# A graph network on one core: node table dropped, edge lists turned on TensorE, gathers issued in waiting pairs

## The reference, cut to what matters

```python
x = _layernorm(x + L0(x, edges))   # two attentions, then a dense update
x = _layernorm(x + L1(x, edges))   # attention with 12 heads of 64
x = _layernorm(x + L2(x, edges))   # normalised neighbour sum, W
x = _layernorm(x + L3(x, edges))   # two such sums, W1 and W2

def gat_conv(x, src, dst, W, a_src, a_dst, bias, H, C, n):    # twice in L0
    h = (x @ W).reshape(n, H, C)
    s_src = (h * a_src).sum(-1)
    s_dst = (h * a_dst).sum(-1)
    e = leaky_relu(s_src[src] + s_dst[dst], 0.2)
    emax = segment_max(e, dst, n)
    ee = exp(e - emax[dst])
    alpha = ee / segment_sum(ee, dst, n)[dst]
    return segment_sum(alpha[:, :, None] * h[src], dst, n).reshape(n, H * C) + bias
```

## Time and profile before

| | us |
|---|---|
| median of 3 runs | 4335.33 |
| the profiled execution | 4339.43 |
| its span, first to last instruction | 4337.6 |
| TensorE matmuls busy in the span | 3720.0 (86%) |
| VectorE | 2597.3 (60%) |
| ScalarE | 1178.5 (27%) |
| GpSimd | 625.8 (14%) |

### The profile page before, as it was taken

The page is one execution under the profiler, slowest core; times in us unless marked ns, Lnnn a source line. Parts: engine busy times, 40 slices in busy tenths (PEclk is TensorE's granted clock), DMA queues, the critical chain, the costliest instruction groups (busy, mean ns, idle before and its releaser), DMA issues. The chain is left out here.

```text
span 4337.6 us, 64010 instructions
## 1 busy us (share of the span) xinstructions
PE 3720.0 (86%) x21454; PEld 3436.2 (79%) x21454; DVE 2597.3 (60%) x4977; ACT 1178.5 (27%) x1691; POOL 625.8 (14%) x640
## 2 busy tenths in 40 slices
PE   6886999699799888026888699999699999699999
PEld 5886999599699544015888399999399999499999
DVE  4765886067142488275999377777244443377777
ACT  2221232122122344003555222222222222222222
POOL 5523000414400000512000400000400000400000
PEclk8987999799899999568999899999899999899999
DMA  4783566346333588116776544444644443666665
GB/s 102 127 189 111 181 192 191 95 133 206 112 104 112 159 250 247 24 55 186 246 251 237 207 155 166 173 172 145 223 161 173 170 167 128 210 220 231 225 225 184
DMA packets 370508, 742.21 MB, mean 171 GB/s; under 512 B 109269, under 2 KB 162215, under 8 KB 370368
## 3 DMA queue, kind: packets, MB, share of 16 engines
q1 hardware_dynamic: 275600, 503.06, 38.1%
q10 hardware_dynamic: 67584, 154.63, 9.1%
q0 software_dynamic: 27184, 82.71, 6.2%
HBM read 444.99 MB, written 301.21 MB: 172 GB/s over the span
## 5 line engine op out<-in xcount | busy, mean ns | idle before, releaser
L666 DVE TENSOR_TENSOR fr_lo<-fr_turned_ps,fr_hi 128x768 fp32r<-128x768 f32 x158 | 150.4, 952 | 339.4 <-ACT fr_hi L1009 331.4
L1139 PE MATMUL fr_prod<-fr_wu_hi,fr_hi 128*128 128x396 f32 x948 | 261.5, 356 | 19.4 <-issue 19.4
L1139 PE MATMUL fr_prod<-fr_wu_lo,fr_hi 128*128 128x396 f32 x948 | 254.2, 348 | 18.3 <-issue 18.3
L1139 PE MATMUL fr_prod<-fr_wu_hi,fr_lo 128*128 128x396 f32 x948 | 252.7, 346 | 18.6 <-issue 18.5
L1139 PE MATMUL fr_prod<-fr_w_hi,fr_hi 128*128 128x396 f32 x948 | 259.2, 354 | 8.8 <-issue 8.8
L1139 PE MATMUL fr_prod<-fr_w_lo,fr_hi 128*128 128x396 f32 x948 | 251.6, 346 | 13.8 <-issue 13.8
L1139 PE MATMUL fr_prod<-fr_w_hi,fr_lo 128*128 128x396 f32 x948 | 250.5, 345 | 11.3 <-issue 11.3
L1009 ACT ACTIVATE fr_hi<-fr_turned_ps 128x768 fp32r<-128x768 f32 x158 | 127.4, 806 | 472.1 <-PE fr_turned_ps L1123 309.6
L2116 DVE SCALAR_TENSOR_TENSOR c3a_y<-c3a_prod,dinv,next_const 128x768 f32<-128x768 f32 x79 | 80.4, 1018 | 289.3 <-PE c3a_prod L2270 289.3
L2270 PE MATMUL c3a_prod<-next_w_hi,c3a_hi 128*128 128x384 f32 x948 | 248.1, 342 | 0.0
L2270 PE MATMUL c3b_prod<-next_w_hi,c3b_hi 128*128 128x384 f32 x948 | 248.0, 342 | 0.0
(11 more groups left out here) (480 smaller groups left out, 8585.4 us busy)
## 6 DMA issues: line engine op xcount, KB each, us to landing
fr_ins<-in_x_dram SPq DMA_DIRECT2D x156, 384.0 KB
h<-fr_outs SPq DMA_DIRECT2D x78, 396.0 KB
u<-fr_outs SPq DMA_DIRECT2D x78, 396.0 KB
up_ut<-u SPq DMA_DIRECT2D x78, 396.0 KB
agg<-fr_zrow SPq DMA_DIRECT2D x78, 390.0 KB
hds_agg<-agg SPq DMA_DIRECT2D x78, 390.0 KB
x<-up_x_o ACTq DMA_DIRECT2D x78, 384.0 KB
hds_row<-x SPq DMA_DIRECT2D x78, 384.0 KB
```

Of the source, the lines that this page charges most:

```text
L666: v.tensor_tensor(lo[:, s2, :, :], turned_ps[:, 0:KC, :], hi[:, s2, :, :].bitcast(F32), ALU.subtract).then_inc(split_done, 1)
L1139: made = nc.tensor.matmul(prods[s2][:, bank, 0:c1 - c0], l[:, s2, s, :], w[:, s, c0:c1], start=(s == 0 and i == 0), stop=(s == KC - 1 and ...
```

## The change

1. The table `nodes`, its 40 gathers and their buffers go. Own loops and dinv of each node become columns 8 and 9 of sc1, so that the gathers of the scores bring them. `sc_o` gets a place for every tile. The rows of sc1 for tiles 0 to 17 are stored later, at SyncE's steps 61 to 78.
2. `sd_c` is not loaded. At `AT_LISTS` TensorE turns both columns of `sd_r`, and VectorE reads the lists from there.
3. In both attentions each pair of gathers of the scores (for a column of 128 edges by src and by dst) waits until the pair in front has landed.
4. `AT_A` goes from 90 to 98, `AT_B` from 127 to 138. The copies of dinv and own loops, and the transpose of these, move from `AT_OWN` into the first attention.

```diff
-AT_A, AT_B = 90, 127
+AT_A, AT_B = 98, 138
...
-    nodes = dram("nodes", (NT * P, 2))
-    sc1 = dram("sc1", (N, 8))
+    sc1 = dram("sc1", (N, 10))
...
 def store(t):
-    sp.dma_start(tile_rows(sc1, t), sc_o[0:n, slot, :, :].rearrange("p h k -> p (h k)")).then_inc(stored[slot], 16)
...
 def step(t):                      # SyncE
+    if AT_NODE + 7 <= t < NT + 4:
+        store_scores(t - 4)
+    if NT - AT_NODE - 3 <= t < NT:
+        store_scores(t - (NT - AT_NODE - 3))
+def store_scores(t):
+    sp.wait_ge(out_ready, 2 * t + 2)
+    sp.wait_ge(node_done, 1)
+    sp.dma_start(tile_rows(sc1, t), sc_o[0:rows_of(t), t, :]).then_inc(sc_stored, 16)
...
-bg.to(AT_NODE + 2)
-sp.wait_ge(node_done, 1)
-sp.dma_start(nodes.rearrange("(t p) k -> p t k", p=P), pt["node"][:, :, :]).then_inc(node_out, 16)
 bg.to(AT_RELOAD)
-sp.dma_start(pt["sd_c"][:, :, :], packed[P:P + NC * P, :].rearrange("(c p) w -> p c w", p=P)).then_inc(reloaded, 16)
...
                                   # GpSimd
-for c in range(SC):
-    rows_from(nodes, pt["nd_src"][:, c, :], g["src_i"][:, c:c + 1], nd_in)
-    rows_from(nodes, pt["nd_dst"][:, c, :], g["dst_i"][:, c:c + 1], nd_in)
...
+pool.wait_ge(sc_stored, 16 * NT)
 for c in range(SC):
-    rows_from(sc1, gt["from_src"][:, c, :], g["src_i"][:, c:c + 1], la.scores_in)
-    rows_from(sc1, gt["from_dst"][:, c, :], g["dst_i"][:, c:c + 1], la.scores_in)
+    if c:
+        pool.wait_ge(la.scores_in[(c - 1) % 2], 32 * ((c + 1) // 2))
+    rows_from(sc1, gt["from_src"][:, c, :], g["src_i"][:, c:c + 1], la.scores_in[c % 2])
+    rows_from(sc1, gt["from_dst"][:, c, :], g["dst_i"][:, c:c + 1], la.scores_in[c % 2])
...                                # the same for lb, from h2
                                   # VectorE
-dve.wait_ge(reloaded, 64)
+dve.wait_ge(reloaded, 48)
+dve.wait_ge(lists_up, 1)
-link(v.tensor_copy(g["src_i"][:, 0:NC], sd_c[:, :, 0]))
-v.tensor_copy(g["dst_i"][:, 0:NC], sd_c[:, :, 1]).then_inc(lists_done, 1)
+link(v.tensor_copy(g["src_i"][:, 0:NC], pb[:, 0:NC]))
+link(v.tensor_copy(pt["dst_c"][:, :], pb[:, 128:128 + NC]))
+v.tensor_copy(g["dst_i"][:, 0:NC], pt["dst_c"][:, :]).then_inc(lists_done, 1)
...
 bg.to(AT_A)
+dve.wait_ge(la.fetched, 1)
+link(v.tensor_copy(g["edge_dinv"][:, :], fs[:, :, 9]))
+link(v.tensor_copy(own_e[:, :], fd[:, :, 8]))
...
                                   # TensorE
+bg.to(AT_LISTS)
+pe.wait_ge(reloaded, 48)
+nc.tensor.transpose(pb[:, 0:NC], pt["sd_r"][:, :, 0], idn)
+nc.tensor.transpose(pb[:, 128:128 + NC], pt["sd_r"][:, :, 1], idn).then_inc(lists_up, 1)
```

More of the change, by code:

```diff
@@ L167, in build @@
         }
-        first_layers(nc, g, a, packed, agg, nodes, h1, sc1, h2, out2, u)
+        first_layers(nc, g, a, packed, agg, h1, sc1, h2, out2, u)
         g["alpha"], g["own_w"] = sb("alpha", [P, NC, H_MAX]), sb("own_w", [P, NC, H_MAX])
@@ L205, in rest_groups, with first_layers @@
                     body(k * 2 + j)
-def first_layers(nc, g, a, packed, agg, nodes, h1, sc1, h2, out2, u):
+def first_layers(nc, g, a, packed, agg, h1, sc1, h2, out2, u):
     with ExitStack() as ctx:
@@ L282, in prep_tiles @@
                 ("pad", [P, (NC + 2) * 2], F32),
-                ("sd_c", [P, NC, 2], F32), ("sd_r", [NC, P, 2], F32), ("prv", [NC, 1], F32), ("nxt", [NC, 1], F32),
+                ("dst_c", [P, NC], F32), ("sd_r", [NC, P, 2], F32), ("prv", [NC, 1], F32), ("nxt", [NC, 1], F32),
                 ("is_last", [NC, P], F32), ("end_r", [NC, P], F32), ("val", [NC, P], F32), ("carry_r", [NC, 1], F32),
-                ("tmp_c", [P, NC], F32), ("deg", [P, NT], F32), ("sq", [P, NT], F32), ("node", [P, NT, 2], F32),
+                ("tmp_c", [P, NC], F32), ("deg", [P, NT], F32), ("sq", [P, NT], F32),
                 ("all_f", [NC, 1], F32), ("all_b", [NC, 1], F32),
-                ("before", [P, P], F32), ("nd_src", [P, NC, 2], F32), ("nd_dst", [P, NC, 2], F32),
-                ("nst", [P, GROUP, 2, 2], F32), ("nix", [P, 2, GROUP], I32), ("scr_p", [P, 8], F32))}
+                ("before", [P, P], F32), ("scr_p", [P, 8], F32))}
         (w1t, w2x, att2), pt, gt = overlay("c", setup_tiles, late_tiles, graph_tiles)
@@ L318, in first_layers @@
                                                                   sem("counted"), sem("offset"), sem("ranks"))
-        packs, slots, hots, hist, deg_done, deg_root, node_done, node_out = (
-            sem("packs"), sem("slots"), sem("hots"), sem("hist"), sem("deg_done"), sem("deg_root"), sem("node_done"), sem("node_out"))
+        packs, slots, hots, hist, deg_done, deg_root, node_done, sc_stored = (
+            sem("packs"), sem("slots"), sem("hots"), sem("hist"), sem("deg_done"), sem("deg_root"), sem("node_done"), sem("sc_stored"))
         zeros, reloaded, rows_done, rows_up, lists_done = (sem("zeros"), sem("reloaded"), sem("rows_done"), sem("rows_up"),
                                                            sem("lists_done"))
-        nd_zero, nd_in, nd_rest, nd_copied, nd_fetched, own_up, own_done = (
-            sem("nd_zero"), sem("nd_in"), sem("nd_rest"), sem("nd_copied"), sem("nd_fetched"), sem("own_up"), sem("own_done"))
+        lists_up, own_done = sem("lists_up"), sem("own_done")
         class Layer:
             def __init__(self, tag):
-                self.zeroed, self.scores_in, self.fetched = sem(tag + "zeroed"), sem(tag + "scores_in"), sem(tag + "fetched")
+                self.zeroed, self.fetched = sem(tag + "zeroed"), sem(tag + "fetched")
+                self.scores_in = [sem(f"{tag}scores_in{j}") for j in range(2)]
                 self.scored, self.up, self.edges, self.edges_up = sem(tag + "scored"), sem(tag + "up"), sem(tag + "edges"), sem(tag + "edges_up")
@@ L347, in stored_by @@
         def stored_by(t):
-            return sum(64 if s < NT else 16 for s in range(t % UNROLL, t + 1, UNROLL))
+            return sum(48 if s < NT else 16 for s in range(t % UNROLL, t + 1, UNROLL))
         @block.sync
@@ L535, in fetch_rest @@
                 rest_groups(pool, g, body)
-            fetch_rest(la, sc1, gt["sst"], 0, 8)
-            pool.wait_ge(la.scores_in, 32 * SC)
+            fetch_rest(la, sc1, gt["sst"], 0, 10)
+            for j in range(2):
+                pool.wait_ge(la.scores_in[j], 16 * SC)
             nc.gpsimd.memset(gt["scr"][:, 1:2], 0.0).then_inc(la.fetched, 1)
@@ L580, in _ @@
             for c in range(SC):
-                rows_from(h2, kept_rows[:, c, 0, :], g["src_i"][:, c:c + 1], lb.scores_in)
-                rows_from(h2, kept_rows[:, c, 1, :], g["dst_i"][:, c:c + 1], lb.scores_in)
+                if c:
+                    pool.wait_ge(lb.scores_in[(c - 1) % 2], 32 * ((c + 1) // 2))
+                rows_from(h2, kept_rows[:, c, 0, :], g["src_i"][:, c:c + 1], lb.scores_in[c % 2])
+                rows_from(h2, kept_rows[:, c, 1, :], g["dst_i"][:, c:c + 1], lb.scores_in[c % 2])
             fetch_rest(lb, h2, stage, 192, 4)
-            pool.wait_ge(lb.scores_in, 32 * SC)
+            for j in range(2):
+                pool.wait_ge(lb.scores_in[j], 16 * SC)
             nc.gpsimd.memset(gt["scr"][:, 1:2], 0.0).then_inc(lb.fetched, 1)
@@ L811, in _ @@
             bg.to(AT_OWN)
[L812 to L817, removed]
             link(v.tensor_scalar(gt["pen_f"][:, :], g["same_f"][:, 0:4 * P], -1.0, NEG, ALU.add, ALU.mult))
@@ L834, in both_ways @@
                 dve.wait_ge(l.edges_up, k)
+                if l is la and k == 1:
+                    link(v.tensor_scalar(own_r[:, :], pb[0:NC, 384:384 + P], 1.0, None, ALU.add))
                 rf, rb = ((pen_rf, pen_rb) if is_max else (g["row_f"], g["row_b"]))
@@ L1196, in hop @@
                 pe.wait_ge(l.edges, k)
+                if l is la and k == 1:
+                    nc.tensor.transpose(pb[0:NC, 384:384 + P], own_e[:, :], ident[:, :])
                 nc.tensor.transpose(pb[0:H, 0:NC], gt["edge"][:, 0, 0:H], idn)
```

23 lines of the change are left out of this document (10 added, 13 removed).

## The result

The changed kernel takes 4210.25 us (median of 4 runs, 4207.33 to 4211.64); the kernel before, on the same chip, 4336.32 (4 runs, 4334.88 to 4338.44). The ratio is 0.9708 [0.9691, 0.9725]: 126 us less. Forecast were 4197 and a range of 4172 to 4245. The profiled execution has a span of 4205.6 us, 132.0 less than before, and a mean granted clock of 0.953 (0.939 before).

A forecast was written before the change was run, and what follows sets the result against it. Four holes, 164 us of a 4337.6 us span, where TensorE starves for x or gets instructions late, were taken to bound it. -33.1 -43.4 +5 -49.4 -38.5 +21 = -138.4 gave 4201, as a median 4197; range 4172 to 4245.

The forecast's parts named there:

- Part 1: Table of nodes dropped: its 8-byte store goes, -33 us; two more score columns cost 0, bound 2 us.
- Part 2: Gathers from the table of nodes dropped: the hole at 340 to 386 us goes, -43 us.
- Part 3: Edge lists turned on TensorE, near tile 31: reload gains 0, VectorE waits for the lists; +5 us, bounds 0 and 8.
- hole 1: TensorE's gap at 205 to 236 us, starving for x behind the 8-byte store of the table of nodes: 33 us.
- Part 4: Gather pairs wait in the first attention: 20 pairs fit up to 5.9 us each; cost 0, bound 2; 49 us returned.
- Part 5: Gather pairs wait in the second attention: 39 us returned, but at p = 4.75 us a pair TensorE waits, +21 us.
- Holes 3 and 4: TensorE's gaps at 774 to 825 and 1119 to 1160 us, instructions late beside back-to-back gathers: 49.4 and 38.5 us.
- Rival B: Pacing doesn't free TensorE's instruction supply, or only in part: 4316 us, half relieved about 4240; chance 0.20.
- hole 2: TensorE's gap at 340 to 386 us, beside back-to-back gathers from the table of nodes: 43.4 us.

The follow-up runs named there:

- run 10: Changed kernel with the store of 128 x 79 pieces of 8 bytes put back at tile 17, read by nobody: 4243.53 us, ratio 1.0088.
- run 1: Changed kernel without the waits between pairs of gathers, all else the same: 4267.62 us, 57 us above the changed kernel.
- run 4: Changed kernel plus 40 unread gathers of 128 rows without a pause in pass c3a, a loop: 4244.40 us, 34 us above the changed kernel.
- run 9: Changed kernel with the reload at tile 28 instead of 26 and the lists turned one tile earlier: 4204.58 us, ratio 0.9991, inconclusive.
- run 12: Changed kernel with a wait after every second pair, AT_A 93, reload at tile 28, lists turned one tile earlier: 4173.03 us, ratio 0.9924.
- run 2: Changed kernel with a wait only after every second pair, four gathers in a row: 4190.00 us, 20 us under the changed kernel.
- run 8: Changed kernel with the first attention from tile 96 instead of 98: 4198.77 us, ratio 0.9981.
- run 11: Changed kernel with a wait only after every fourth pair, eight gathers in a row: 4181.16 us, ratio 0.9938.
- run 3: Changed kernel with each pair waiting for the pair before the last, two pairs under way: 4212.64 us (4191.94 to 4223.05).
- run 5: Changed kernel plus 40 unread plain GpSimd transfers of 128 rows of 40 bytes in pass c3a, without waits: 4212.47 us, ratio 1.0010.
- run 7: Changed kernel plus 40 unread gathers of 64 rows each in pass c3a, without waits: 4210.89 us, ratio 1.0010.
- run 6: Changed kernel plus 40 unread gathers of 32 rows each in pass c3a, without waits: 4211.14 us, ratio 1.0009.

## Why the prediction was right, and where it was off

**Part 1, right.** SyncE no longer has a long load near 197 us, and tile 17 starts 7.18 us after tile 16. -33.3 us came against -33.1, and run 10 puts it back with one store.

**Part 2, right in size, its cause by likeness.** -43.4 us was taken. The gathers of the table were never tried with pauses. That they slowed TensorE as a train, and not in another way, is argued from their form (128 rows, 1.30 us apart), which is that of runs 1 and 4, and not shown. TensorE's first wait for "issue" came there at 340.64 us, after 8 gathers, where the others needed 12 to 14.

**Part 3, right.** +5 was taken, +5.5 came, and in the order foreseen: VectorE stands 3.93 us (forecast 4), its low part comes late, and the tiles 31 and 32 take 10.78 and 8.67 us.
```profile
300.73 0.06 DVE L708 MEMSET src_i<- 128x4 int32 x1 [3.93 <-PE fr_pb L1145]
...
310.11 0.94 DVE L648 TENSOR_TENSOR fr_lo<-fr_turned_ps,fr_hi 128x768 fp32r<-128x768 f32 x1
```

**Not foreseen: +4.0 us at tiles 26 and 27.** With hole 1 gone TensorE reaches the reload 35 us earlier, and the scatters that it waits for do not. SyncE stands from 250.68 to 260.42, with the loads of x queued behind:
```profile
250.27 0.41 SPq L401 DMA_DIRECT2D sc<-fr_sc_o  x1
260.42 0.30 SPq L418 DMA_DIRECT2D fr_sd_r<-packed  x1
```
```profile
264.64 0.56 DVE L633 BATCH_NORM_STATS2 fr_stats<-fr_ins 128x6 f32<-128x384 f32 x1 [7.76 <-DMA fr_ins<-in_x_dram]
```
```profile
270.12 1.51 PE L1105 MATMUL fr_turned_ps<-ident,fr_xn 128*128 128x128 f32 x6 [2.46 <-DVE fr_lo L648]
```
The prediction asked what was late next for the gathers, and not for this queue. Runs 9, 10 and 12 bear it out: with hole 1 back (run 10) the 4.0 us are gone, and with the reload two tiles later (runs 9 and 12) too. How much is lost varies from trace to trace, because the last scatter's issue ends anywhere from 253.4 to 263.8 us where there is no hole 1: in runs 1 and 2 it ended at 255.2 and 253.4, and nothing was lost; in run 8 at 263.8, and 5.0 us were.

**Part 4, right.** It was said that 20 pairs fit up to 5.9 us each. They took 5.05, and nobody waited. -49.5 us came against -49.4.

**Part 5, the step that was mis-sized.** Its form was right: one wait of VectorE at tile 138 (35.1 us long), and room for p = 3.8. I took a landing of 2.0 us and p = 4.75, and +21 us; p was 5.15 and the price 26.7 + 1.3 = 28.0 over steps of 7.18 (27.4 over the 7.61 and 7.35 that tiles 139 and 140 take in run 11 without the wait). The forecast's own sum, 14.0 + 20 p + 3.5 - 93.5, gives 27.0 with the measured p, and 29 with the 2 us at the low clock, so p accounts for the miss. By the sum of the forecast, 5.15 - 2.3 - 0.45 is a landing of 2.4 us. The waits of the list average 55.0 / 19 = 2.9 us with the start of the next issue in them, where the forecast had 2.45. Each 0.1 us of a landing is paid 20 times. The error was to think the stage as good as quiet, since it moves only x and u: that is 149 GB/s by the stretches table, and the other bound, 3.32 us behind four scatters, was nearer than it looked. The rule weighed there, a fixed 2.0 us of the Trainium skill, DMA: Bandwidth & Descriptors, "Anatomy of one DMA", would have made the part free. Waits of 2.4 to 4.2 us behind an issue of 1.0 in this stage speak against taking it for a transfer beside others.

**Holes 3 and 4, the mechanism.** Two statements stood in one sentence, "TensorE gets its instructions late while gathers come without a pause". What the trace shows of it, waits for "issue" that pauses take away, holds in runs 1, 2 and 11. That it is late because of fetching is refuted by run 4. The cure was forecast by likeness with stretches that have pauses, and not from a known cause; that the cause named beside it was wrong cost nothing here, which is luck. Rival B doubted the cure, and is refuted by the 102.00 of 102 us; its remark that the holes would have another cause than fetching was right.

**The sum.** Forecast were -138.4 us; the terms came to -33.3 - 37.9 - 49.5 - 37.5 + 28.0 = -130.2. With the 4.0 not foreseen that is -126.2. Of the 12.2 us between, 7.0 are part 5 and 4.0 the tiles 26 and 27. The span's -132.0 has 5.8 us more. 2.3 of them are at the start-up, for which I have no cause (tile 0 alone moves by up to 4 us from run to run), and 3.4 between tiles 86 and 122, of which 2.5 are the four steps moved out of that row. The medians differ by 126.1, so that the terms meet them so closely is in part luck.

**What stays open.** Why trains of indexed gathers with 128 rows hold up TensorE's issue. One reading that fits, and is not shown, is a supply of something that refills with time: 8 to 14 gathers of 128 rows use it up, half the rows never do, and a pause of 2 us or more after each 2, 4 or 8 gathers keeps it, where 0.7 us does not. Whether single pauses count or the mean rate was not separated: run 3 slowed after 38 us at 1.46 us a gather (first attention), and run 11 never did in some 62 us at 1.54. The bytes of a row do not matter much: rows of 8 bytes (hole 2), 32 (hole 3) and 784 (hole 4) all made a hole. Where between 64 and 128 rows it starts was not tried, nor a train of plain transfers longer than 21 us.

## What to carry to other kernels

Where TensorE waits for "issue" at a low granted clock and few bytes move, look for a train of indexed gathers on GpSimd, and break it with a wait after each 4 to 8 gathers (8 is near the limit: hole 2 began after 8). A wait after each 2 cures it as well, but every wait pays a landing of 2 to 4 us. Before such waits are added, compute the room from the producer's tile to the consumer's and divide it by the number of waits, with the landing under load. When a stall is taken away, ask of every queue, and not only of the engine that was cured, what now comes before its data is there.

## What the runs showed of the hardware that I had not expected

- 40 indexed gathers of 128 rows in a row, 1.30 us apart, cost TensorE 46 and 38 us (run 1) and 31 (run 4), from 12 to 14 gathers after the first on. In run 4 they did so in matmuls that TensorE had run in earlier turns of the same loop, with no instruction packets. 40 gathers of 64 rows in the same place left the length of the pass as it was (539.2 us against 539.5).
- A transfer of GpSimd of 128 rows of 40 bytes takes 0.53 us to issue when it is plain (run 5) and 1.00 + 0.30 when it is indexed; indexed with 64 rows it is 0.94 (run 7) and with 32 rows 0.92 (run 6), so here the price is per instruction and hardly per row.
- A store of 10,112 pieces of 8 bytes takes 0.38 us to issue and holds the next load in the same queue for 24.41 us (run 10).
